# The one-hot comparison of a graph-network kernel written with a second output, the row sum of its result

## What is computed

```python
pri = -jnp.arange(N)                        # lower-numbered neighbours first
scores = jnp.where(A != 0, pri, -inf)
vals, idx = jax.lax.top_k(scores, 25)       # the first 25 neighbours of each node
feats = jax.vmap(lambda x, i: x[i])(X, idx) # their feature rows
agg = feats.max(axis=2)                     # elementwise maximum over the 25
...
out = relu(concat([X, agg]) @ W + b)
```

## Time and profile before

| | |
|---|---|
| median of 3 runs | 2067.38 us |
| the profiled execution's own time | 2068.06 us |
| its span, first to last instruction | 2066.3 us |
| granted TensorE clock, mean | 0.919 |
| busy share PE, DVE, ACT, POOL | 82%, 70%, 49%, 76% |
| chain that ended last: PE, POOL, DVE | 34%, 26%, 17% |
| comparison, line 1290 | 139 instructions, 173.0 us busy |

### The profile page before, as it was taken

How to read it: one execution, slowest core, us unless ns; L and a number is a source line. 1 busy time by engine, 2 the same in 40 slices (tenths; PEclk the granted TensorE clock), 3 DMA queues, 4 the chain that set the end, 5 groups by cost and what they waited for, 6 DMA issues and landing times.

```text
span 2066.3 us, 29885 instructions
## 1 busy us (share of the span) xinstructions
PE 1690.6 (82%) x9198; PEld 1279.0 (62%) x9252; DVE 1441.8 (70%) x3522; ACT 1016.2 (49%) x1353; POOL 1567.2 (76%) x2257
## 2 busy tenths in 40 slices
PE   2756698887889698897889798896989888895877
PEld 1545486665766577575666577574766677574755
DVE  5766588657876588667977588766887579745631
ACT  3010465457555465556645465555655474551252
POOL 5888887888888888788888888888887888882000
PEclk9878789997999899998999889998999989997899
DMA  6321322424232522323333442333223342311010
GB/s 159 85 72 45 73 75 69 122 76 111 77 104 81 118 73 71 123 77 96 73 102 92 98 103 72 114 84 97 74 74 119 76 105 63 101 45 44 1 62 11
DMA packets 155329, 171.27 MB, mean 83 GB/s; under 512 B 103709, under 2 KB 121002, under 8 KB 155178
## 3 DMA queue, kind: packets, MB, share of 16 engines
q1 hardware_dynamic: 119594, 96.43, 17.4%
q0 software_dynamic: 35584, 72.95, 13.5%
HBM read 144.65 MB, written 4.19 MB: 72 GB/s over the span
## 4 chain that ended last, share of the span: by engine, by line
PE 34%; POOL 26%; DVE 17%; issue 9%; ACT 5%; DVEq 5%; DMA 3%; SPq 1%; POOLq 0%; ACTq 0%
POOL gathered L521 20%; PE big L942 7%; POOL pause L526 6%; PE spare L840 6%; PE big L1036 3%; DVEq L72 3%; PE side L840 2%; PE side L1052 2%; DMA adj_t<-adj_bf 2%; PE big L933 2%; DVE pooled L1243 2%; PE big L866 1%; DVE keys L1143 1%; DVE hot L1290 1%; DVE neg_max L1444 1%
## 5 line engine op out<-in xcount | busy, mean ns | idle before, releaser
L521 POOL DMA_INDIRECT gathered<-in_x_dram,rows x1112 | 1179.0, 1060 | 262.0 <-issue 167.6
L526 POOL MEMSET pause<- 32x256 bf16 x1112 | 383.5, 345 | 44.2
L840 PE MATMUL spare<-hot,x_part 128*128 128x512 f32 x1200 | 316.1, 419 | 41.2 <-DVE hot L1290 37.8
L840 PEld LDWEIGHTS spare<-hot,x_part 128*128 128x128 f32 x1200 | 236.5, 201 | 99.5 <-issue 31.4
L1243 DVE TENSOR_REDUCE pooled<-gathered 128x128 f32<-128x2304 f32 (+1 forms) x56 | 223.0, 3982 | 69.2 <-DMA gathered<-in_x_dram,rows 66.5
L582 ACT ACTIVATE hot<-running,minus_count 128x2048 fp32r<-128x2048 bf16 x105 | 209.7, 1997 | 49.6 <-PE spare L840 49.6
L942 PEld LDWEIGHTS big<-values,probs_t 128*128 128x128 f32 x1792 | 219.4, 199 | 8.9
L942 PE MATMUL big<-values,probs_t 128*128 128x129 f32 x1792 | 222.2, 283 | 0.9 <-issue 0.7
L585 ACT ACTIVATE hot<-hot,plus_one 128x2048 fp32r<-128x2048 f32 x105 | 210.3, 2002 | 3.4
L840 PE MATMUL side<-hot,x_part 128*128 128x512 f32 x560 | 152.3, 421 | 59.3 <-ACT hot L585 40.9
L1290 DVE TENSOR_SCALAR hot<-running 128x2048 fp32r<-128x2048 bf16 x139 | 173.0, 1267 | 30.7 <-PE spare L840 18.9
(11 more groups left out here) (195 smaller groups left out, 2559.0 us busy)
## 6 DMA issues: line engine op xcount, KB each, us to landing
adj_in<-in_adj_dram SPq DMA_DIRECT2D x128, 512.0 KB
gathered<-in_x_dram,rows POOLq DMA_INDIRECT x1112, 2.5
xs<-in_x_dram SPq DMA_DIRECT2D x8, 512.0 KB, 4.7
out_dram<-xs SPq DMA_DIRECT2D x8, 512.0 KB, 3.3
adj_t<-adj_bf SPq DMA_TRANSPOSE x64
packed_t<-group_bits SPq DMA_TRANSPOSE x28
w_sb<-in_L_gnn_W_dram SPq DMA_DIRECT2D x1, 128.0 KB
w_sb<-in_L_gnn_W_dram SPq DMA_DIRECT2D x2, 64.0 KB
```

The costliest lines, as they stand in the source:

```text
L521: (late_gathered if late else rows_gathered[t % RING]).raised_by(pool.indirect_dma_start(out=gathered[:, t % RING, k * C:(k + 1) * C], out ...
L526: last = nc.gpsimd.memset(pause[quarter:quarter + 32, k // (4 * PAUSED), :], 0.0)
L840: last = nc.tensor.matmul(pick_bank(b, q), x_parts[part][:, m, :], hot[c][:, m % per, :], start=(m == 0 and part == 0), stop=(m == T - 1 a ...
```

## The change

The comparison gets a second output: beside `hot` it writes the number of ones of each partition into one column of a new tile `hot_sum`. The operation given for the reduction is an addition. Nothing reads `hot_sum`. No other instruction, wait or order is changed, and `hot` has the same values.

```diff
         hot = [sb(f"hot{c}", [P, T // CHUNKS, N // 2], F32R) for c in range(CHUNKS)]
+        hot_sum = sb("hot_sum", [P, CHUNKS])
...
                     hot_ready.raised_by(nc.vector.tensor_scalar(
                         hot[c][:, :, :], running[:, per * c:per * (c + 1), :],
-                        float(wanted(b, q)), None, ALU.is_equal))
+                        float(wanted(b, q)), None, ALU.is_equal, ALU.add, accum_out=hot_sum[:, c:c + 1]))
```

## The result

The changed kernel took 2119.6 us in the median of 4 runs (2116.2 to 2121.6), the kernel before 2067.1 us in 4 (2059.3 to 2072.3). The ratio is 1.0256, with the interval 1.0231 to 1.028: **slower by 52.6 us**, where 72 were forecast. The profiled execution took 2120.16 us, its span is 2118.4 us, and PE's mean granted clock is 0.916, against 0.919 before.

A forecast was written before the change was run, and what follows sets the result against it. A graph was taken as bound about 180 us by DVE and PE in turn, then some 55 us by POOL. Graph 0's 29.9 us plus the later graphs' 42.3 make 72.2, forecasting 2140 us, range 2118 to 2168.

The forecast's parts named there:

- The rate: DVE's comparison of 2048 columns slows from 0.50 to 1.04 ns a column, to about 2.30 us, 1.03 us more a chunk.
- Rival 1: The comparison keeps its rate and only a readout of 0.17 us is added: about 2074 us, chance 5%.
- rival 3: The sum is paced as the pooling reduction, 2.6 us more a chunk: about 2290 us, chance 3%.
- The readout: Reading the sum on DVE adds 0.17 us behind each comparison, making the price 1.20 us a chunk.
- rival 4: Mechanism as forecast, but the readout waits (1.4 us a chunk, 2159 us) or hides wholly (1.03, 2126 us); within the forecast's 89%.
- Graph 0's part: Ahead of the loop, 48 chunks cost 57.6 us, idle times hide some; 29.9 us slower, with no helpful idle time behind.
- The sign for it: In the changed kernel, graph 0's last pick should be some 28 us later.
- the forecast's four terms: DVE idle times hiding graph 0's cost: waits for PE 15.2 us, wait at 55.74 2.4, at 132.19 1.2, gather at 196.87 8.9.
- A later graph: Of 13 chunks, picks 4, 5, 7 chunk 1, 8 and 10 chunk 0 count: +7.3 us less 1.3, +6.0, seven times 42.3.
- The sign at gat 2: DVE's wait of 3.07 us at gat 2, behind pick 7 chunk 0, should shrink to 1.9.
- POOL's release: The slower comparison no longer holds POOL: pick 13's gather falls from 2.24 to 0.95 us, worth 1.3 us a graph.
- Rival 2: It gets faster: the new form frees POOL's gathers and costs DVE almost nothing, about 2049 us; chance 3%.

The follow-up runs named there:

- The probe: Seven single DVE comparisons ahead of the program, in the kernel summing only the six uncovered chunks a later graph; that kernel took 2166.5 us, ratio 1.0336.
- pair of profiles: Profiles of the kernel before and of the whole change, both from the second set: 2065.0 us (ratio 0.9996) and 2114.1 us (ratio 1.0247).
- first two profiles: Profiles of the kernel before and of the changed kernel from the first measurement, 2067.1 and 2119.6 us, ratio 1.0256.
- whole and later graphs: Second set: the sum in all comparisons, 2114.1 us, ratio 1.0247, and only in the later graphs, 2099.2 us, ratio 1.0159, against the kernel before.
- second set: Undisturbed runs of the kernel before (2067.8 us), itself again (ratio 0.9996), whole change (1.0247), later graphs alone (1.0159) and pick 13 alone (0.9956).
- filler: Kernel before with a 960-column DVE reduction ahead of each old-form comparison: 2161.0 us, ratio 1.0277, and again 2167.4 us, ratio 1.0299.
- first set: Disturbed runs, kernel before 2100.6 us: sum in graph 0 alone (ratio 1.0117), later graphs alone (1.0431), pick 13 alone (1.0102), and the filler (1.0277).
- later graphs alone: Sum only in the later graphs' comparisons (91 of 139), against the kernel before: 2189.3 us, ratio 1.0431; repeated in the second set, 2099.2 us, 1.0159.
- graph 0 alone: Sum only in graph 0's comparisons (48 of 139), against the kernel before: 2125.6 us, ratio 1.0117; repeated in the third set, 2123.1 us, 1.0113.

## Why the prediction was right, and where a step of it failed

**The rate: right.** The loss was put at 1.03 us from the slope of the folding instructions. It is 2279 - 1267 = 1.01 us by the means after and before. The probe shows the slope itself, 1.04 ns. That the MAX8 groups run at this rate too is an agreement of numbers; the record doesn't show that the cause is the same. Rival 1 (rate kept) and rival 3 (3.7 us) fell by the first row of the changed kernel.

**The readout: mis-sized.** "I take 0.17 us" was to stand for a short instruction that overlaps only a little. It takes 82 ns, and the next instruction starts with it. The price is 1.0 us, not 1.20. This is the low end of rival 4, for which 2126 us was worked out.

**Graph 0's part: the step that failed** is "Behind it stands no idle time that helps". Behind the last comparison stood DVE's wait of 7.53 us for the last gather, ahead of the maximum for which PE waited 10.34 us. I had looked at what PE does next, not at what DVE still waits for ahead of it. With the price of 1.03 the forecast's own working gave 24 us for this part; less the 7.5 that is 16.5. The pair of profiles shows 18.8, the first two profiles 18.1 (layer 1's first step at 238.26 before and 256.40 after), the difference of whole and later graphs 15 to 18.

The sign for it, graph 0's last pick 28 us later, came out as 26.3, and told nothing of what came through behind it. That it came so near is two errors that cancel. With 1.03 us a chunk the forecast's working gives 47 x 1.03 - 25 = 23 there. But ahead of that pick DVE's idle time shrank only from 47.6 to 26.4 us in the pair, that is by 21.1, where the forecast's four terms (15.2, 2.4, 1.2 and 8.9) add up to 27.7, or 25 at the lower price. The wait for `packed_t`, which was to hide 1.2 us, even grew, from 14.1 to 14.9. These 3 us more, and 0.8 us less in PE's counting behind the pick (12.3 us from its first matmul to layer 1's first step before, 11.5 after), turn the 16.5 into 18.6, near the 18.8 measured.

**A later graph: right in kind, mis-sized.** +6.0 was forecast; with the measured price the same working gives 0.1 + 6 x 1.01 - 1.3 = 4.9. Measured are 31.5 / 7 = 4.5 alone. From the growth of the spans less graph 0's part it is (52.1 - 18.1) / 7 = 4.9 between the first two profiles and (48.2 - 18.8) / 7 = 4.2 between the pair of the second set. Together with pick 13's gain the six chunks on the path cost (31.5 + 8.7) / 42 = 0.96 us each. Part of the rest can be seen at pick 4, where the two chunks hold DVE from 1030.81 to 1035.40 us after and from 995.60 to 998.40 before, that is 4.59 against 2.80 us: 0.90 a chunk, since the old form was itself slow there, as at 1000.72.

Where the time went can be read from the starts of DVE's chunks in the two pairs of profiles. The table is worked out from the traces. An entry is the change of the time from the start of the named chunk to the start of the one in the next line, summed over the seven graphs, in us; the forecast stands with 1.01 us a chunk. For pick 13 the time runs to the next graph's pick 1, in the last graph to the end.

| DVE's chunks | forecast | before, after | pair of the second set |
|---|---|---|---|
| pick 1 | 0.7 | -1.0 | -1.8 |
| pick 4, both | 14.1 | 11.5 | 12.8 |
| pick 5 | 7.1 | 5.8 | 5.7 |
| pick 7, chunk 0 | 0 | -2.0 | -3.0 |
| pick 7, chunk 1, and pick 8 | 14.1 | 14.7 | 14.7 |
| pick 9, both | 0 | 5.4 | 0.6 |
| pick 10, both | 7.1 | 9.6 | 10.9 |
| pick 13, both, and POOL's part | -9.1 | -9.6 | -14.0 |
| sum | 34.0 | 34.4 | 25.9 |

An entry of the same kernel differs by up to 5 us from one execution to the next (pick 9 in the two changed ones), so only the larger differences say something. The chunks of picks 4, 5, 7 (chunk 1) and 8, which were counted in full, come out so within 3 us. Pick 7's chunk 0 cost nothing, but the reason given was read in one graph: the wait of 3.07 us at gat 2 stands in three of seven graphs, and where it is missing nothing that the forecast names covers the chunk. It came out right by luck there. Pick 9 is covered for the most part. The second chunk of pick 10 is not covered fully: over the seven graphs the two cost 2.5 to 3.8 us more than one chunk each. The sign at gat 2, 3.07 us shrinking to 1.9, came out as 0.85 in that graph; since this wait comes and goes between graphs, one graph's value tests little.

**POOL's release: right.** Gathers in graph 0's part went from 1237 to 951 ns, and at pick 13 the release alone is worth 8.7 us (3.5 to 14.7) against 9.1 forecast. The Trainium skill, SBUF — State Buffer, section "Who interferes with whom", says that a DVE instruction with one SBUF input outside the two-port modes doesn't contend with GpSimd. The trace agrees: 2.24 us with the old form beside the gather, 0.95 with the new. What the release is worth within the whole change no run tells: the filler was meant to, and both its runs are disturbed.

**The other rivals.** Rival 2 (faster) had the right mechanism and the wrong size for the whole: at 1.0 us a chunk it loses. At the one place where POOL is the path and DVE is not, it is what happens. The 105.7 us that POOL has less to do went into waits for DVE, 121.0 and 97.6 us in the rows above. PE's clock fell a little, as said: in the second set from 0.922 to 0.918 by the medians of the runs. What that costs was not taken apart.

The sum made anew from the measured terms: 18.8 + 29.4 = 48.2 us on the pair's spans, 2063.1 to 2111.3. It is 24 us below the forecast's 72.2. In graph 0's part the price accounts for 5.9 (29.9 to 24) and the wait for the gather for 7.5, together 2.3 us more than the 11.1 that are missing there; this is the other side of the hidden waits above. In the later graphs the price accounts for 7 x 6 x 0.19 = 8.0 of 12.9 us. The other 4.9 us are not in the first two profiles, where the later graphs grew by 52.1 - 18.1 = 34.0 us, what the working gives at the measured price, so they are within what differs from one execution to the next.

**How much of it was luck.** The measured 2119.6 us lies in the range of 2118 to 2168, but 1.6 us from its end and below the 2126 that the forecast named as the lowest of its own case. The increase was 52.6 us where 72 stood. It came inside by the width left for a miscounted chunk, not because graph 0's part was understood; in the second set the changed kernel took 2114.1 us.

## What to carry to other kernels

Asking a DVE comparison for its accumulator turns it from 0.5 to 1.0 ns a column, so it belongs only where DVE has idle time behind it. There, if POOL's gathers are the path, this slower form is the faster one, since it doesn't hold them: the new form at pick 13 alone is the best version here (0.9956). When an engine comes later, follow it through all its own waits up to the instruction that the next engine takes from it, and not only to the end of the stretch that is changed; each wait for something that doesn't move hides its full length. A cover that was read in one graph has to be looked up in the others before it is multiplied by seven. An experiment on an effect of one per cent needs the kernel before and the whole change in the same set of runs.

## What the runs showed of the hardware that was not expected

**Types don't matter to the summed form.** Into bf16, the plain comparison of 1024 columns takes 0.47 us and the summed one 1.22, so there the sum costs 0.75 us, against 0.46 into f32.

**Hand-overs from PE come late in some sets.** In the first set, pick 13 alone, all engines in order of time at 1456 us:

```profile
1456.12 0.75 PE L990 MATMUL big<-ident,pooled 128*128 128x128 f32 x4
...
1458.27 1.31 SPq L388 DMA_TRANSPOSE adj_t<-adj_bf  x1
...
1464.24 0.69 DVE L1423 TENSOR_TENSOR probs_t<-big,best_t 128x512 f32<-128x512 f32 x1 [8.38 <-remote]
```

PE's transposes end at 1456.87 by the profile, and DVE, which waits for them, starts 7.4 us later. DVE's waits named "remote" add up to 68 us in 21 places in this run, 79 in 24 in the later graphs alone, 38 in 18 in graph 0 alone, and there are none on DVE in the four kernels of the second set nor in the first two profiles. On ACT the name alone is no sign: its step `running` has such waits of 192 us in the first profile of the kernel before too, in which 54 of 9252 matmul records are missing. The chain by engine of the same kernel in the first and in the second set:

```profile
PE 48%; DVE 17%; issue 14%; ACT 8%; DVEq 6%; another core or an unknown queue 4%; POOL 3%; DMA 1%; SPq 1%; ACTq 0%; POOLq 0%
```

```profile
PE 39%; POOL 23%; DVE 15%; issue 8%; ACT 6%; DMA 4%; DVEq 3%; SPq 1%; POOLq 0%; ACTq 0%
```

The transposes of the adjacency by DMA run at that place, but I have no run that takes them away, and no profile of the kernel before from a disturbed set. What delays the hand-over, and why some kernels lose more by it than the kernel before, stay open.
